# Token-major projection and mix in a hybrid block kernel: pairs of small matmuls in array halves, transpositions over two banks, single signals in the column stage

## The reference

```python
x = x + conv(group_norm(x))          # the part that is changed
t = tokens(x)
t = t + attention(layer_norm(t))
t = t + haar_ffn(layer_norm(t))

def conv(x):                          # x is already group-normalised, called gx in the kernel
    xn = x / (norm(x) / sqrt(256) + 1e-8)
    u = silu(xn @ W_u.T + b_u)        # 512 channels
    v = silu(xn @ W_v.T + b_v)
    y = irfft2(rfft2(v, 112 x 112) * rfft2(g))[:56, :56]   # long convolution over the image
    return (u * y) @ W_o.T + b_o + x
```

## Time and profile before

| | |
|---|---|
| runs before, median (range) | 6520.24 us (6500.59 to 6524.92), 3 runs |
| the profiled execution's own time | 6512.99 us |
| its span, first to last instruction | 6511.2 us |
| TensorE busy, mean granted clock | 5960.6 us (92%), 0.923 |
| VectorE, ScalarE, GpSimd busy | 4122.5, 2801.3, 2428.0 us |
| project, columns, mix | 905 to 1714, 1714 to 3400, 3400 to 4725 us |

### The profile page before, as it was taken

The page is one execution under the profiler, slowest core; times in us unless marked ns, Lnnn a source line. Parts: engine busy times, 40 slices in busy tenths (PEclk is TensorE's granted clock), DMA queues, the critical chain, the costliest instruction groups (busy, mean ns, idle before and its releaser), DMA issues. The chain is left out here.

```text
span 6511.2 us, 94031 instructions
## 1 busy us (share of the span) xinstructions
PE 5960.6 (92%) x29000; PEld 4504.0 (69%) x29000; DVE 4122.5 (63%) x6520; ACT 2801.3 (43%) x5030; POOL 2428.0 (37%) x1405
## 2 busy tenths in 40 slices
PE   8999869999799999999989999999888888887999
PEld 5666556666555555555549999999866776765998
DVE  5555567777688888888875555555555555555444
ACT  4454328888533333333333333333333333332444
POOL 0000025555388888888872222222201111111332
PEclk9999979999899999999998888888789999998999
DMA  0111276666544444444445555565422222222333
GB/s 34 34 34 34 76 180 219 212 217 219 164 140 139 140 139 140 139 140 138 141 132 166 166 172 174 164 182 155 147 90 88 83 85 85 85 85 77 100 100 94
DMA packets 338044, 831.67 MB, mean 128 GB/s; under 512 B 32169, under 2 KB 134473, under 8 KB 322160
## 3 DMA queue, kind: packets, MB, share of 16 engines
q1 hardware_dynamic: 322626, 779.16, 39.7%
q10 hardware_dynamic: 15344, 51.50, 2.3%
HBM read 470.57 MB, written 359.98 MB: 128 GB/s over the span
## 5 line engine op out<-in xcount | busy, mean ns | idle before, releaser
L621 POOL TENSOR_TENSOR co_prod<-co_direct 111x512 f32<-111x512 f32 x448 | 772.3, 1724 | 343.2 <-DVE co_cross L600 337.2
L559 ACT ACTIVATE co_y_out<-co_y_ps 112x512 f32<-112x512 f32 x448 | 268.2, 599 | 1043.0 <-PE co_y_ps L505 1038.2
L599 DVE TENSOR_TENSOR co_direct<-co_v_ps,co_spec 111x1024 f32<-111x1024 f32 x448 | 546.0, 1219 | 232.8 <-PE co_v_ps L129 216.2
L622 POOL TENSOR_TENSOR co_prod<-co_cross 111x512 f32<-111x512 f32 x448 | 629.4, 1405 | 0.0
L882 POOL TENSOR_TENSOR pr_gx<-pr_x_in,pr_gn 112x1024 f32<-112x1024 f32 x56 | 143.2, 2557 | 1107.9 <-DMA pr_gn<-gn_rows 1105.4
L1569 POOL TENSOR_TENSOR at_t<-at_t,at_p_bias 112x1024 f32<-112x1024 f32 x56 | 132.0, 2363 | 1113.6 <-DMA at_t<-t_tiles 1113.6
L504 PE MATMUL co_y_ps<-co_prod,co_col_inv 111*112 111x512 f32 x896 | 472.2, 608 | 78.8 <-POOL co_prod L622 76.9
L600 DVE TENSOR_TENSOR co_cross<-co_v_ps,co_spec 111x1024 f32<-111x1024 f32 x448 | 542.8, 1212 | 0.0
L1218 PE MATMUL mx_y_ps<-mx_row_inv,mx_y_in 112*128 112x56 f32 x3584 | 525.8, 321 | 0.0
L1218 PEld LDWEIGHTS mx_y_ps<-mx_row_inv,mx_y_in 112*128 112x128 f32 x3584 | 522.4, 237 | 0.1
L129 PE MATMUL co_v_ps<-co_v_high,co_col_fwd_high 112*111 112x512 f32 x896 | 509.2, 568 | 1.4 <-DVE co_cross L600 1.4
(11 more groups left out here) (251 smaller groups left out, 15915.3 us busy)
## 6 DMA issues: line engine op xcount, KB each, us to landing
v_rows<-pr_rows_out SPq DMA_DIRECT2D x56, 1792.0 KB, 9.1
co_v_in<-v_rows SPq DMA_DIRECT2D x448, 224.0 KB
y_rows<-co_y_out SPq DMA_DIRECT2D x448, 224.0 KB
mx_y_in<-y_rows SPq DMA_DIRECT2D x56, 1792.0 KB, 15.8
at_n_raw<-n_t SPq DMA_DIRECT2D x112, 448.0 KB, 3.3
kern_rows<-kr_rows_out SPq DMA_DIRECT2D x28, 896.0 KB
st_x_in<-x SPq DMA_DIRECT2D x56, 448.0 KB, 10.6
pr_x_in<-x SPq DMA_DIRECT2D x56, 448.0 KB, 8.7
```

The costliest lines, as they stand in the source:

```text
L559: nc.scalar.activation(y_out[:, b, :], y_ps[b % 2][:2 * SIDE, :], ACT.Copy).then_inc(y_ready, 1)
L599: nc.vector.tensor_tensor(direct[b % 2][:], v_ps[b % 2][:POINTS, :], spec[i][:, :2 * WIDE], ALU.mult)
L621: nc.gpsimd.tensor_tensor(prod[b % 2][:, :WIDE], direct[b % 2][:, :WIDE], direct[b % 2][:, WIDE:], ALU.subtract)
L622: nc.gpsimd.tensor_tensor(prod[b % 2][:, WIDE:], cross[b % 2][:, :WIDE], cross[b % 2][:, WIDE:], ALU.add).then_inc(combined, 1)
```

## The change

Project and mix become token-major: tokens stay on the partitions behind the matmul, with the two image rows of a tile at partitions 0 to 55 and 64 to 119 (GAP 64, SPAN 120).

In project GpSimd only makes gx, for groups of four chunks that have four buffers (cleared once, since 8 partitions between the rows are never loaded). gx itself is transposed; the inverse norm is applied behind the product by VectorE, in the operation that adds the bias (`bias` has it as its scalar), and 8 of its columns are stored per two chunks to inv_cols for mix. xn_t is no longer made or stored. v stays plain fp32: `row_pass` is one fp32 matmul per image row over its own 56 partitions, two per tile, into two PSUM banks.

In columns `direct` and GpSimd's subtraction raise semaphores of their own (`real_terms`, `real_ready`).

In mix gx is made again from x and the group norm's rows on GpSimd, transposed half by half in one PSUM bank (turn_ps[1], shared with the transpositions of the norm's result), and the gate is computed with tokens on the output partitions. `inverse_rows` has the 56 x 112 matrix as stationary operand and y as the moving one: per tile two fp32 matmuls of 512 columns, each to 56 output partitions at 0 or 64 of one bank. The product is then transposed in the other bank (turn_ps[0]). Work on a chunk stretches over four steps (`later`, `after`, `now`, `before`, `before2`), normalising moves from VectorE to ScalarE, and x and y are loaded with x first and y in four parts. The stage's unchanged tail and the rest of the new steps are left out below.

```diff
+GAP = 64
+SPAN = GAP + SIDE
+GROUP = 4
...
-    fwd = np.zeros((TILE, 2, ROWS))
-    fwd[:SIDE, 0], fwd[SIDE:, 1] = row, row
+    fwd = np.zeros((128, ROWS))
+    fwd[:SIDE], fwd[GAP:SPAN] = row, row
...
-                    done(pe, combined, n)
+                    pe.wait_ge(real_ready, n + 1)
                     buffer_free(pe, y_ready, n)
                     nc.tensor.matmul(y_ps[b % 2][:2 * SIDE, :], col_inv[:, 0, :], prod[b % 2][:, :WIDE], start=True, stop=False)
+                    done(pe, combined, n)
                     nc.tensor.matmul(y_ps[b % 2][:2 * SIDE, :], col_inv[:, 1, :], prod[b % 2][:, WIDE:],
                                      start=False, stop=True).then_inc(inv_mm, 1)
...
+                        pool.wait_ge(real_terms, k * BATCH + b + 1)
+                        buffer_free(pool, inv_mm, k * BATCH + b)
+                        nc.gpsimd.tensor_tensor(prod[b % 2][:, :WIDE], direct[b % 2][:, :WIDE], direct[b % 2][:, WIDE:],
+                                                ALU.subtract).then_inc(real_ready, 1)
                         done(pool, multiplied, k * BATCH + b)
-                        buffer_free(pool, inv_mm, k * BATCH + b)
-                        nc.gpsimd.tensor_tensor(prod[b % 2][:, :WIDE], direct[b % 2][:, :WIDE], direct[b % 2][:, WIDE:], ALU.subtract)
                         nc.gpsimd.tensor_tensor(prod[b % 2][:, WIDE:], cross[b % 2][:, :WIDE], cross[b % 2][:, WIDE:],
...
-                def scale(s, u, first=False):
-                    g = 2 * s + u
-                    pool.wait_ge(inverted, s + 1)
-                    if not first:
-                        pool.wait_ge(xt_mm, g - 1)
-                    each = inv[:, u * TILES:(u + 1) * TILES].unsqueeze(2).to_broadcast([TILE, TILES, CH])
-                    nc.gpsimd.tensor_tensor(xn[u][:], gx[u][:], each, ALU.mult).then_inc(xn_ready, 1)
...
-                def row_pass(s, u, t):
-                    n = (2 * s + u) * TILES + t
-                    pe.wait_ge(low_v, n + 1)
+                def row_pass(s, j, t):
+                    n = (s * GROUP + j) * TILES + t
+                    done(pe, v_ready, n)
                     buffer_free(pe, row0_out, n)
                     buffer_free(pe, row1_out, n)
                     for r in range(2):
-                        last = product(nc, row_ps[t % 2][r][:ROWS, :], [w[:, r, :] for w in row_fwd],
-                                       [x[:] for x in v_parts[t]], start=True, stop=True)
+                        side = slice(r * GAP, r * GAP + SIDE)
+                        last = nc.tensor.matmul(row_ps[t % 2][r][:ROWS, :], row_fwd[side, :], v[t][side, :], start=True, stop=True)
...
+                def gate(s, j, t, rows_before):
+
+                    done(act, biased, (s * GROUP + j) * TILES + t)
+                    act.wait_ge(row_mm, rows_before)
+                    nc.scalar.activation(v[t][:], v_pre[t % 2][:], ACT.Silu).then_inc(v_ready, 1)
...
+                def bias(s, j, t):
+                    n = (s * GROUP + j) * TILES + t
+                    dve.wait_ge(v_mm, n + 1)
+                    buffer_free(dve, v_ready, n)
+                    nc.vector.scalar_tensor_tensor(out=v_pre[t % 2][:], in0=v_ps[t % 2][:SPAN, :],
+                                                   scalar=inv[:SPAN, j % GROUP * TILES + t:j % GROUP * TILES + t + 1],
+                                                   in1=v_bias[:SPAN, :], op0=ALU.mult, op1=ALU.add).then_inc(biased, 1)
...
+                def load_x(s, u, first=False):
+                    g = s * 2 + u
+                    if not first:
+                        sp.wait_ge(gate_ready, s * 8 + (u - 1) * TILES)
+                        sp.wait_ge(resid_ready, s * 2 + (u - 1))
+                    sp.dma_start(x_in[u][:], d["x_tiles"][g]).then_inc(x_loaded[u], 16)
+                    sp.dma_start(gn[u][:].rearrange("p a c -> p (a c)"), d["gn_rows"][g].to_broadcast([TILE, 2 * CH])
+                                 ).then_inc(x_loaded[u], 16)
+                    sp.dma_start(inv_in[u][:], d["inv_cols"][s][:, u * TILES:(u + 1) * TILES]).then_inc(x_loaded[u], 16)
...
+                def load_y(s, u, t, first=False):
+                    if not first:
+                        sp.wait_ge(y_mm, s * 8 + (u - 2) * TILES + t + 1)
+                    row = (s * 2 + u) * CHUNK_ROWS + 2 * t
+                    sp.dma_start(y_in[u][:, 2 * t:2 * t + 2, :], d["y_rows"].rearrange("k b i c -> k (b i) c")[:, bass.ds(row, 2), :]
...
+                def normalise(s, u, first=False):
+                    g = s * 2 + u
+                    pool.wait_ge(x_loaded[u], s * 48 + 48)
+                    if not first:
+                        pool.wait_ge(xt_mm, s * 4 + (u - 1) * 2)
+                    nc.gpsimd.tensor_tensor(gx[u][:], x_in[u][:], gn[u][:, 0:1, :].to_broadcast(each), ALU.mult).then_inc(scaled_x, 1)
+                    pool.wait_ge(scaled_x, g + 1)
...
+                def residual(s, u, first=False):
+                    g = s * 2 + u
+                    pool.wait_ge(gx_ready, g + 1)
+                    if not first:
+                        pool.wait_ge(t1_ready, s * 4 + (u - 1) * 2 + SLOTS)
+                    nc.gpsimd.tensor_tensor(resid[u][:], x_in[u][:], o_bias[:].unsqueeze(1).to_broadcast(each),
+                                            ALU.add).then_inc(resid_part, 1)
+                    pool.wait_ge(resid_part, g + 1)
...
+                def inverse_rows(s, u, t):
+                    n = (s * 2 + u) * TILES + t
+                    pe.wait_ge(y_loaded[u][t], s * 16 + 16)
+                    buffer_free(pe, gated_ready, n)
+                    for r in range(2):
+                        last = nc.tensor.matmul(y_ps[t % 2][r * GAP:r * GAP + SIDE, :], row_inv[:], y_in[u][:, 2 * t + r, :],
+                                                start=True, stop=True)
+                    last.then_inc(y_mm, 1)
...
+                def turn_gated(s, u, t):
+
+                    n = (s * 2 + u) * TILES + t
+                    done(pe, gated_ready, n)
+                    once_past(pe, low_mixed, n)
+                    for c in range(BLOCKS):
+                        last = nc.tensor.transpose(turn_ps[0][:, c * 128:c * 128 + SPAN],
+                                                   gated[t % 2][:, c * 128:(c + 1) * 128], ident[:SPAN, :SPAN])
+                    last.then_inc(turned, 1)
...
+                def step(before2, before, now, after, later):
+                    if now:
+                        gate_mm(*now, 2)
+                    if before:
+                        turn_gated(*before, 3)
+                        output_mm(*before, 2)
+                    if after:
+                        pe.wait_ge(low_x, number(after) * HALVES + 1)
+                        turn_x(*after, 1)
+                    if now:
+                        inverse_rows(*now, 0)
+                        gate_mm(*now, 3)
+                        turn_gated(*now, 0)
+                    if before:
+                        output_mm(*before, 3)
+                    if before2:
+                        if after:
+                            pe.wait_ge(low_x, number(after) * HALVES + 2)
+                        turn_norm(*before2, 0)
+                    if now:
+                        inverse_rows(*now, 1)
+                        if after:
+                            gate_mm(*after, 0)
+                        turn_gated(*now, 1)
+                        output_mm(*now, 0)
+                    if before2:
+                        pe.wait_ge(nt0_ready, number(before2) + 1)
+                        turn_norm(*before2, 1)
+                    if now:
+                        inverse_rows(*now, 2)
+                        if after:
+                            gate_mm(*after, 1)
+                        turn_gated(*now, 2)
+                        output_mm(*now, 1)
+                    if later:
+                        if before2:
+                            pe.wait_ge(nt1_ready, number(before2) + 1)
+                        else:
+                            pe.wait_ge(low_x, number(after) * HALVES + 2)
+                        turn_x(*later, 0)
+                    if now:
+                        inverse_rows(*now, 3)
...
-                def inverse_rows(s, u, first=False):
-                    g = 2 * s + u
-                    pe.wait_ge(y_loaded[u], s * 16 + 16)
-                    for c in range(BLOCKS):
-                        if not first:
-                            pe.wait_ge(mixed_ready, (g - 1) * BLOCKS + c + 1)
-                        for r in range(CHUNK_ROWS):
-                            last = nc.tensor.matmul(y_ps[c][:, r * SIDE:(r + 1) * SIDE], y_in[u][:, r, c * 128:(c + 1) * 128],
-                                                    row_inv[:], start=True, stop=True)
...
+                def take_x(s, u, h):
+                    act.wait_ge(xt_mm, (s * 2 + u) * HALVES + h + 1)
+                    if h == 0:
```

(19 more changed lines are left out.)

919 lines of the change are left out of this document (481 added, 438 removed).

## The result

The changed kernel takes 6292.65 us (median of 4 runs, 6288.44 to 6297.26), the kernel before on the same chip 6510.41. The ratio is 0.9664, 95% interval 0.964 to 0.9689: 218 us less. The profiled execution has a span of 6289.6 us where the one before had 6511.2, 221.6 less. Forecast were 6165 us and 351 less: the direction was right, the gain came out at about six tenths. 6293 us lies outside the forecast's own range of 6075 to 6240, to which I gave 0.70, and inside 6070 to 6310, the range that was widened for rivals 2 and 3.

A forecast was written before the change was run, and what follows sets the result against it. TensorE's order was taken to bound the three stages; in mix two loops were to set the period. Gains of 189, 84 and 78 us sum to 351, giving 6165 us; own range 6075 to 6240 (0.70), widened to 6070 to 6310.

The forecast's parts named there:

- Rival 2: Project and mix: each switch of tiling costs a full pipeline tail, 0.17 us; kernel near 6260 us; chance 0.07.
- rival 3: Mix: the clock stays at 0.81 because of short transpositions and stalls; period 23.5 us, kernel 6294 us; chance 0.08.
- Loop A: Mix, statistics: from x's transposition through normalising and gating to the product's transposition and TensorE's next x transposition, 20.6 us.
- loop B: Mix, load: x's load waits for the last gate, then lands and passes GpSimd before its transposition; 20.3 to 21.1 us.
- the signs that I had named for a wrong prediction: Pairs running in sequence, a table load where none was expected, or a loop longer than walked.
- the three terms: Expected stage gains: project minus 189 us, columns minus 84 us, mix minus 78 us.
- The pair at 0.86 us: Project: two fp32 row matmuls on array halves overlap, taking 0.86 us together, against 1.72 us in sequence.
- switch cost: Project: changing between array halves and full matmuls costs at most 0.09 us at eight switches; half taken, 0.35 us a chunk.
- 1.5 of the 2.0 us: Columns: earlier GpSimd subtraction and TensorE's shorter wait save 1.5 us per frequency, of 2.0 unexplained; minus 84 us.
- rivals 4 and 5: Mix: x lands in 8.6 us, kernel 6403 us, chance 0.05; or in 16.5 us, kernel 6845 us, chance 0.03.
- My 21.2 us: Mix: period taken per chunk, with 60 us of fill giving 1247 us for the stage.

The follow-up runs named there:

- same-half kernel: Changed kernel with both row transforms of a project tile reading partitions 0 to 55: 6487.43 us, project 857.9 us.
- The early start alone: Changed kernel with GpSimd still subtracting after the first product, but TensorE waiting for both GpSimd operations as before: 6324.96 us, columns 1597.1 us.
- one moved line: Changed kernel with VectorE's mix(now, 0) moved ahead of residual(before, 0) and low_part_x(after, 1): 6212.09 us, mix 1278.2 us.
- the kernel with both edits in mix: Changed kernel with VectorE's mix(now, 0) moved up and mix's inverse norms on a semaphore of their own: 6107.22 us, mix 1167.8 us.

## Why the prediction was right, and where it was off

**The total: inside the wide range only, and in part by luck.** Loops A and B in mix are longer than I walked them, which is one of the signs that I had named for a wrong prediction, and each of the three terms came out beyond its own range or at its edge: project 134 us against 136 to 200, columns 113 against 50 to 110, mix a growth of 35 against at most 20. 6293 us is near rival 3's 6294, and the period of 23.5 us is the one that it named, but its cause did not come: it had the clock low over the whole stage, because of short transpositions.

**Project, overlap: right.** The pair at 0.86 us was a choice between two bounds, and the same-half kernel confirms it to 0.01.

**Project, switch cost: the term that was mis-sized.** I took 0.35 us a chunk from one row of attention, the first matmul after the row groups. Measured is 4 x 0.37 = 1.5 us, so 11.27 us for TensorE, in place of the 10.15 that I summed and the 10.35 that I took; 56 x 0.92 = 51 us of the gain went there. The row showed one end of the switch only; the timeline after shows three pieces (0.09 ahead of the pair, 0.19 in it, 0.10 behind it). My second rival had this, with 0.17 at each of eight switches, and its 76 us in project came as 83 (56 x 4 x 0.37). I gave it 0.07. The Trainium skill, "TensorEngine Tiling (Array Packing)", section "Tiling Modes", says that changing the mode drains the engine; I had set that rule aside for one row. The trace agrees with it in that every change costs; that it is a drain no run shows. Rival 2's other 40 us, on loop A, did not come: without the slow clock TensorE's part of the loop is 11.5 us, as I had it with switches. The table loads, DMA and ScalarE hid as I had said: TensorE has no wait in the steady part of the stage.

**Columns: right, and a little more.** I took 1.5 of the 2.0 us a frequency that were not explained by TensorE's work; all of it went (27.5 us against my 27.6 of pure work). The stage's 113 us are 3 more than my upper bound. The early start alone gives 85 us, the 84 that I had said; the last part came from the two signals together.

**Mix, the two loops right, the size and the binding one wrong.** Loop A binds, with the wait at the place named; loop B is next, 22.2 us against my 20.3 to 21.1; x lands in 3.9 us, so rivals 4 and 5 fell. My 21.2 us went by loop B, which I had as the longer one at its upper end, and I had said that with loop A alone binding mix would be faster than forecast; it is slower. Loop A is 23.4 us in the chunk shown, not 20.6. On the ScalarE and VectorE side the error is 1.2 us, most of it the inversion and shift: 3801.20 to 3802.58, 1.4 us, where I had 0.45, because I priced an operation on 4 elements as if nothing could hold it up. On TensorE's side it is 1.5 us, and all of it is the slow clock after the stall: twelve output matmuls in 2.5 us in place of 1.5, four transpositions in 0.88 (0.48), a pair in 1.15 (1.00). What came is a short dip behind the loop's own wait: in this chunk 2.4 us of waiting cost 1.5 more. I had also let the wait stand as a given, and not asked whether tile 0's product had to stand behind the low part of x on VectorE. That order was no part of the data's need, and it set the loop.

**Where the expected gain went, then.** Of the 129 us that are missing, 51 went to the array's switches and 113 to mix, less the 29 that columns gave beyond my term and some 6 outside these periods. The 113 are 56 x (23.5 - 21.2) = 129 of the period, by loop A, less some 16 of fill. Of the 113 one moved line gives back 74, and it uncovers loop B.

Some sums of the prediction don't come out as written, by little: ScalarE's terms in project add up to 8.8 us and not 9.2, and rival 3's stretch of loop A is 11.5 x 0.96 / 0.81 = 13.6 us and not 13.9. Neither changes the forecast.

## What to carry to other kernels

Small matmuls in array halves overlap in full here, but a round trip between the whole array and halves costs about 0.4 us, so place them in groups. Where several loops close over a step, list them all with their lengths: removing one is worth only its distance to the next, and an edit that measures as nothing may be worth a hundred us behind another, or may hide a gain and a loss of the same size. Look in each in-order engine for an operation that waits behind one that it doesn't need.

## What the hardware showed that I had not expected

- VectorE's variance and shift, on 112 x 4 elements in SBUF, take 0.16 to 0.17 us, or up to 2.04 us in the rows shown when GpSimd is in an operation, and end with that operation. Not every VectorE operation does: the reciprocal at 3801.20, as small and in the middle of GpSimd's operation, takes 0.18 us, and so do all 37 that start inside one from 3300 to 4300 us, where each of the 37 shifts behind them ends with GpSimd's. Holding GpSimd back by one wait was worth 73 and 52 us. The Trainium skill, "SBUF — State Buffer", section "SBUF: two separate sides", says that VectorE and GpSimd share a pair of ports that one of them holds for a whole instruction, and that VectorE asks for it with two inputs in SBUF or in a mode that uses two ports. For the shift, which has two inputs in SBUF, the trace agrees; the variance has one, and whether it runs in such a mode no run shows.
- In columns it is GpSimd's operation that is stretched, and the change moved which one: the subtraction took 1727 ns in the mean before and takes 1286 now, the addition 1410 before and 1899 now. The trace shows what it goes with, VectorE's low part of the next v (or of the taps), an operation with two inputs in SBUF:

```profile
2491.94 1.63 DVE L583 TENSOR_TENSOR co_v_low<-co_v_in,co_v_high 112x1024 fp32r<-112x1024 f32 x1
2492.44 2.27 POOL L629 TENSOR_TENSOR co_prod<-co_cross 111x512 f32<-111x512 f32 x1
```

Of 320 additions from 1900 to 3000 us the 200 that start inside such an operation take 2.26 to 2.29 us and end 1.14 to 1.16 us after it; the other 120 take 1.27 to 1.30, also the 80 of them that start inside `direct` or `cross`, which have one input in PSUM.
- Behind the stall of 2.4 us in the chunk shown TensorE ran at 1.2 GHz for about 3 us; with stalls of 0.8 us a chunk, in the kernel with both edits in mix, the granted clock was 1.00 from 3300 to 4200 us.
- Going from fp32r to fp32 matmuls on the whole array costs nothing that the timeline shows; the round trip to halves and back costs 0.37 us.
